# A graph-attention pass on TensorE: the matmuls of zeros ahead of the waits are taken out

## The reference

```python
h = (x @ W).reshape(N, H, D)
a_src = jnp.einsum('nhd,hd->nh', h, att_src)
a_dst = jnp.einsum('nhd,hd->nh', h, att_dst)
alpha = a_src[src] + a_dst[dst]
alpha = jax.nn.leaky_relu(alpha, NEG_SLOPE)
alpha = jnp.exp(alpha - amax[dst])
alpha = alpha / (denom[dst] + 1e-16)
msg = h[src] * alpha[:, :, None]
out = jax.ops.segment_sum(msg, dst, num_segments=N)
```

## Time and profile before

| | us |
|---|---|
| median of 3 launches | 10336.57 |
| lowest, highest | 10336.55, 10338.63 |
| the profiled launch, device time | 10338.73 |
| its span, first to last instruction | 10336.9 |
| the attention pass in it, first to last fill | 175.5 to 2948.7 |

### The profile page before, as it was taken

How to read it: one execution, slowest core, us unless ns; L and a number is a source line. 1 busy time by engine, 2 the same in 40 slices (tenths; PEclk the granted TensorE clock), 3 DMA queues, 4 the chain that set the end, 5 groups by cost and what they waited for, 6 DMA issues and landing times.

```text
span 10336.9 us, 260758 instructions
## 1 busy us (share of the span) xinstructions
PE 7025.2 (68%) x70494; PEld 5117.6 (50%) x70495; DVE 4776.3 (46%) x12912; ACT 1865.3 (18%) x3800; POOL 4554.0 (44%) x4467
## 2 busy tenths in 40 slices
PE   5888778778735666666778866666676454555677
PEld 4666556556522221113454545665675454444676
DVE  4555555555468877774443333333232332222333
ACT  2333333332211334551000000000000000000000
POOL 3777656555410000004661045435554765553754
PEclk7899888888868988998889977777777776667788
DMA  3444333333310122335556665665566676556676
GB/s 68 95 94 92 83 89 83 82 80 72 74 49 25 75 87 112 137 135 172 165 172 183 179 207 194 208 217 178 204 223 207 220 273 212 199 201 228 205 253 228
DMA packets 973370, 1566.22 MB, mean 152 GB/s; under 512 B 499841, under 2 KB 621441, under 8 KB 966402
## 3 DMA queue, kind: packets, MB, share of 16 engines
q1 hardware_dynamic: 485762, 1244.14, 34.2%
q0 software_dynamic: 150016, 196.43, 9.4%
q10 hardware_dynamic: 337280, 122.87, 4.6%
HBM read 1337.91 MB, written 225.00 MB: 151 GB/s over the span
## 4 chain that ended last, share of the span: by engine, by line
PE 38%; issue 18%; DVE 15%; POOL 12%; DVEq 9%; DMA 6%; ACT 2%; ACTq 0%; SPq 0%; POOLq 0%
PE ps_turn L977 15%; POOL ARENA L662 12%; PE ps_out L824 6%; PE ps_turn L932 4%; DMA ARENA<-counts 3%; PE ps_pair L824 2%; DMA ARENA<-edge_attr 2%; PE ps_turn L797 2%; DVE ARENA L1766 2%; DVE ARENA L1764 2%; PE ps_turn L735 1%; PE ps_out L739 1%; DVEq L1771 1%; PE ps_pair L859 1%; PE ps_out L1014 1%
## 5 line engine op out<-in xcount | busy, mean ns | idle before, releaser
L977 PE MATMUL ps_turn<-ARENA 128*128 128x192 bf16 (+2 forms) x28812 | 2722.3, 261 | 708.7 <-DVE DSUM L1916 322.7
L977 PEld LDWEIGHTS ps_turn<-ARENA 128*128 128x128 bf16 x28812 | 2286.0, 105 | 1134.9 <-issue 824.1
L662 POOL DMA_INDIRECT ARENA<-table_sage,idx x1920 | 1866.9, 972 | 1510.0 <-issue 993.2
L662 POOL DMA_INDIRECT ARENA<-table_gat,idx x1568 | 1728.8, 1103 | 1054.9 <-DMA idx<-src_r 557.2
L932 PE MATMUL ps_turn<-ARENA 128*128 128x392 bf16 (+1 forms) x4204 | 1058.5, 356 | 676.3 <-DVE ARENA L1766 375.4
L662 POOL DMA_INDIRECT ARENA<-table_dev,idx x480 | 469.8, 979 | 1671.3 <-ACT idx L1177 1527.9
L1764 DVE TENSOR_SCALAR ARENA<-ARENA 128x784 bf16<-128x784 f16 (+1 forms) x2102 | 1007.2, 479 | 357.1 <-issue 230.9
L932 PEld LDWEIGHTS ps_turn<-ARENA 128*128 128x128 bf16 (+1 forms) x4204 | 332.4, 100 | 1402.3 <-issue 1357.7
L662 POOL DMA_INDIRECT ARENA<-table_gine,idx x480 | 469.8, 979 | 945.4 <-issue 691.3
L1159 ACT ACTIVATE ARENA<-ps_turn 128x784 f32 x784 | 646.1, 824 | 1077.5 <-PE ps_turn L932 1077.1
L1916 DVE TENSOR_REDUCE DSUM<-ps_turn 128x64 f32<-128x192 f32 (+2 forms) x686 | 263.6, 384 | 1171.0 <-PE ps_turn L977 1074.4
(11 more groups left out here) (303 smaller groups left out, 6913.7 us busy)
## 6 DMA issues: line engine op xcount, KB each, us to landing
ARENA<-counts SPq DMA_DIRECT2D x1764, 448.0 KB
counts<-ARENA SPq DMA_DIRECT2D x49, 3136.0 KB, 9.0
ARENA<-counts SPq DMA_DIRECT2D x588, 224.0 KB
ARENA<-dst_b SPq DMA_DIRECT2D x393, 256.0 KB
ARENA<-edge_attr ACTq DMA_DIRECT2D x392, 128.0 KB
ARENA<-table_sage,idx POOLq DMA_INDIRECT x1920
ARENA<-table_gat,idx POOLq DMA_INDIRECT x1568
nodes_dev<-table_rows ACTq DMA_DIRECT2D x14, 672.0 KB
```

Source lines behind the costliest of these rows:

```text
L662: pool.indirect_dma_start(ps["buf"][:, s, c, 0:ps["row"]], None, ps["table"][:, :], bass.IndirectOffsetOnAxis(idx[:, s, c:c + 1], 0)).then ...
L977: last = pe.matmul(ps_dense[half][:, 0:n], RING[:, b, :], XP[:, b, :], start=(b == PIECE_AT[pieces[0]]), stop=(j == pieces[-1] and b == PI ...
```

## The change

`fill`, its three calls and the PSUM corner that it wrote are removed. The matmuls of zeros at L852 and L863, which open and close the accumulation of `expand`, stay. No wait, no semaphore and no other instruction is changed, on any engine.

```diff
-        ps_fill = ps_turn[:, 2048 - P:2048]
...
-            def fill(n):
-
-                for _ in range(n):
-                    pe.matmul(ps_fill, ZERO[:, :], ZERO[:, :], start=True, stop=True)
-
...
                 def expand(g, lo, hi):
 
-                    fill(5)
                     pe.wait_ge(logit_ready, g + 1)
                     pe.matmul(ps_exp_all[:, 0:C * 2 * H], ZERO[:, :], ZERO[:, 0:C * 2 * H], start=True, stop=False)
                     with pe.Fori(lo, hi) as t:
                         pe.reg_add(spread, spread, 1)
-                        fill(5)
                         pe.wait_ge(nodehot_ready, pe.snap(spread, min_val=1, max_val=GROUPS * TILES))
...
                         further_tiles(*last)
                         if gat:
-
-                            fill(6)
                             pe.wait_ge(messages_ready, g * 2 + 2)
```

## The result

The changed kernel takes 10382.62 us (median of 6 launches, 10363.60 to 10397.17), the kernel before 10339.26 (6 launches). The ratio is 1.0037, 95% interval 1.0026 to 1.0049: slower by 0.26% to 0.49%. The forecast was 10367 us, slower, in a range of 10255 to 10480. The profiled launch took 10378.96 us, 40.2 more than that of before.

A forecast was written before the change was run, and what follows sets the result against it. GpSimd was taken to bound the attention pass up to 830 us, its consumers after that. Profiled launch 10338.7 - 89 (fills' time) + 120 (clock) + 0 (first part) = 10369.7, median 10367 us; range 10255 to 10480.

The forecast's parts named there:

- the clock holds: Rival, attention pass: TensorE stays busy enough without fills, so only the 89 us gain is left, 10248 us; chance 0.22.
- most sums at 1.2 GHz: Rival, attention pass: half of the other 304 sums join the slow ones, 334 us lost, 10582 us; chance 0.08.
- it does nothing: Rival: fills' time goes to edge DMA and VectorE, clock loss falls into the round's end; within 20 us; chance 0.15.
- The clock term: Attention pass from 830 us: granted clock falls from 0.86 to 0.78 without fills, 120 us lost.
- the second part: Attention pass from 830 to 2949 us: consumers are the bound, GpSimd waits 557 us; the change acts here.
- The busy share: TensorE's busy share from 830 us on: falls from 0.78 to 0.59 without fills, at the old length.
- the later passes: Passes without fills, used to bound the clock: busy 0.54 to 0.68 goes with clocks of 0.71 to 0.78.
- the forecast's own conversion: From 830 us: clock lower by 0.08 moves 339 us to 1.2 GHz, half of its matmul time lost, 97 to 149 us.
- The gain: Attention pass from 830 us: half of the fills' 178 us on the chain comes back, 89 us, bounds 0 and 178.
- The six ahead of the sum: Fills at the sum's wait, L813: almost wholly covered by the edge features' DMA.
- The limit by the DMA: One-tile groups at full clock: edge DMA holds two groups to at least 7.1 us, 3.55 each.
- The first part: Attention pass up to about 830 us: GpSimd's gathers are the bound, priced at 0, bounds 12 us gain and about equal loss.

The follow-up runs named there:

- e8: Kernel before with the two calls of five fills widened to 256 columns from 128, the six ahead of the sum kept; 10403.71 us, ratio 1.0059.
- e2: Kernel before without the six fills ahead of the sum's wait, the two calls of five kept; 10378.30 us, ratio 1.0039.
- e1: Kernel before without the two calls of five fills (logits' and nodehot waits), the six ahead of the sum's wait kept; 10346.15 us, ratio 1.0006.
- e4: Kernel before without the two calls of five fills, and twelve in place of six ahead of the sum's wait; 10335.63 us, ratio 0.9996.
- e7: Kernel before without the two calls of five fills, and eight of 256 columns ahead of the sum's wait; 10337.51 us, ratio 0.9999.
- e3: Kernel before with fills of 4 columns in place of 128, in calls of 11, 11 and 13 for 5, 5 and 6; 10665.22 us, ratio 1.0313.
- e5: Kernel before with fills of 4 columns in place of 128, calls still of 5, 5 and 6; 10438.78 us, ratio 1.0089.

## Why the prediction was right, point by point

**Direction and mechanism: right.** Two opposite terms, the fills' time given back and the clock lost, with the second larger. e8 raises both (more clock, more time), e2 shows the sixes' part (less clock, little given back). The rival "the clock holds" fails with 0.79 where it asked for 0.85 or more; "most sums at 1.2 GHz" fails with 0.79 where it asked for less than 0.7; "it does nothing" asked for less than 20 us, and the interval of the ratio starts at 27.

**The clock term: right in size.** 0.78 was taken for the second part, 0.79 measured; 120 us lost was taken, the fp32 matmuls alone show 127 (1177 against 1050). Part of that is luck. The busy share was put at 0.59, for which the later passes gave 0.73; it came out at 0.69 (1537 of 2217), since sums at the low clock keep TensorE busy longer, and 0.78 was the highest of those rows, taken by judgement. And by the forecast's own conversion a fall of 0.07 is 307 us more at 1.2 GHz, of which the fp32 matmuls would have lost 87; they lost 127. The clock falls behind a wait of 1.65 us within a round, and the sum in which it falls takes 4.09 us (the rows at 886 to 896 above). The section "HAM oscillation — how this bites in real kernels" of the Trainium skill, page "TensorE: Matmul & The Clock Gate", which was cited against the change, speaks of bursts shorter than the waits between them. Here the direction agrees with it, but the matmuls ahead of this wait had run for 7.6 us (882.39 to 889.97), so that the case goes beyond what the section says; not every wait does it, as the 0.79 shows.

**The gain: right in sum, wrong in how it comes about.** 89 us were taken for the second part (from 830 us on), half of the most that was possible; 102 are what the rows above leave there (from 760 on), 127 less 25. The half was a choice between two bounds, so that it came out near is partly luck. The six ahead of the sum were called almost wholly covered: e2 bears it out for the most part (3 to 15 us, and 24 to 28 by e1 against the change). But the groups with one tile at full clock were to take 3.5 to 3.7 us, held by the edge DMA. The group shown takes 2.90, which is TensorE's own pace without fills (2.94 was worked out). It is no exception: from one L845 to the next, 102 groups with one tile ran wholly at full clock in the changed kernel's pass, 67 of them in less than 3.2 us and 6 in 3.4 to 3.75. The limit by the DMA is there, but it acts on two groups together, as the forecast's sum for two groups (7.1 us) had it: one runs in 2.90, the next waits for its edge features, as in the rows at 886 to 896. What failed here is the even share of 3.55 for each, and the full clock behind the wait that it took for granted: the two took 9.66 us.

**The first part: the step that failed.** It was priced at 0, because GpSimd filled the stretch. GpSimd's gathers are the bound there only as long as the groups are summed faster than it gathers. With a clock of 0.81 they no longer are: the gathers' share of the chain fell from 40% to 15%, and the part grew by 13 us, a little beyond the loss of about 12 that was given as the bound. GpSimd itself kept its pace (429 gathers in 598 us against 417 in 585, rows above): at the end of the part it was 12 gathers, three groups, further ahead of the sums. It was the clock rather than the loss of the fives: e1 and e4 both have none, and their fp32 matmuls, counted to the same 880th, end at 769 and 758 us, with clocks of 0.84 and 0.88. Windows of e1 and of e4, fp32 matmuls alone:

```profile
175.00:769.00 594.00, 325.01 (x880) 0.84 0.44 95
```

```profile
175.00:758.00 583.00, 304.21 (x880) 0.88 0.45 97
```

With that, the sum -89 + 120 + 0 = +31 reads -102 + 127 + 13 = +38 by the rows (the growth of the two parts), against 40.2 in the profiled launch and 43 in the medians.

**What stays open.** Why a matmul of 4 columns pushes the next one out by half as much as one of 128; the small matmuls at L859 do the same (12 in 0.31 us, 26 ns each). Why the clock falls behind some pauses and not behind others. And how far the single terms of the table can be trusted: its two columns of rests differ by some 20 us in e7, and more launches with a profile would be needed to tell the sixes' 3 from 28.

## What to carry to other kernels

A filler matmul in front of a wait has a price and a yield, and they depend on its place: in front of a wait that ends late anyway (a DMA that lands 3 us later) it holds the clock at a small price, as long as it fits into that wait (the second six of e4 no longer did), in front of one that is often already satisfied it delays what is behind it by its own length. Ask of each one which wait it stands at before taking all of them out, or all of them in. And an engine that is made faster between two waits may only wait longer at the second; where its clock depends on its being busy, it then pays for the wait a second time.

## What the runs showed of the hardware that was not expected

TensorE's program is loaded anew in each round when the loop's body gets too long. With 35 matmuls of zeros for each group (e3) the instruction queue moved 7.29 MB in the launch, in the other runs 0.43 to 0.49, and in places the chain then waits up to 8 us. The launch is 226 us longer than e5, whose fills are of the same size and fewer; how much of that the loading costs is not shown, since the 19 further fills and a lower clock (0.77 against 0.80) are in it too and TensorE is idle no longer than in e5. Where between 16 and 35 it begins was not tried.

The granted clock need not fall in the pause itself: in the rows at 886 to 896 it was 1.00 through a pause of 1.65 us, and fell 0.68 us after TensorE had gone on. Most of the sum behind it then ran at 1.2 GHz, though TensorE was busy throughout.
